# Layer-1 experts: the order of the layer-norm scales, who normalises the first tokens, and where the shared output is kept

## The chip, the cores and the metric

The kernel runs on one core of a Trainium2 chip. The metric is the time of one execution on the device in microseconds (us); three executions of the kernel before took 2908.03, 2914.95 and 2923.42 us, so its median is 2914.95 us. Engines are TensorE (PE; PEld is its weight load), VectorE (DVE), ScalarE (ACT), GpSimd (POOL) and SyncE (SP), whose queue issues most of the DMAs.

## The reference

Twelve sublayers work on `x`, 4096 tokens of 128 numbers in float32. The change touches the third kind, which is called twice, around the layer-1 attention:

```python
x = x + 0.5 * _L1_ffn_ref(_layernorm(x, axis=-1), ...)

logits = x @ router_w.T                        # 64 experts
probs = softmax(logits); topk_w, topk_ids = top_k(probs, 8); topk_w /= sum(topk_w)
pos = (how many earlier (token, choice) pairs went to the same expert)
valid = pos < 64                               # an expert takes its first 64 tokens
y = (silu(xb @ w_gate) * (xb @ w_up)) @ w_down # per expert, xb its 64 tokens
routed = segment_sum(y * topk_w)
shared = (silu(x @ ws_gate) * (x @ ws_up)) @ ws_down
return routed + shared
```

`_layernorm(x)` is `(x - mean) / sqrt(var + eps)` per token.

## The kernel before, in words

`l1_ffn` (L1057 to L1611) is one stage: each engine has its own program, ordered by hand, and engines wait for each other by semaphores. All of `x` stays in SBUF as `core.x`: 32 tiles of 128 tokens, in 8 chunks of 4 tiles. The stage runs in three parts.

**Choosing.** VectorE makes means and variances of all tokens (`ln_scales_dve`), GpSimd raises the variances to the power -0.5 chunk by chunk (`ln_scale_pool`, L162): chunks 0 and 1, then two iotas and twelve small memsets, chunks 2 and 3, two memsets (`table_rows`' pad and `zero`), chunks 4 to 7. For each chunk VectorE's `shift(c)` (L1287) makes the product -mean times scale; ScalarE's `normal(c)` (L1443) normalises four tiles with it; TensorE's `turn_x(c)` (L1520) transposes them; ScalarE's `keep_xnt(c)` (L1449) copies the result out; TensorE multiplies by the router (`logits`, L1532); VectorE's `choose(c)` (L1313 to L1322) finds the 8 largest of 64 logits per token, the shifted logits and a mask; ScalarE's `exp(c)` (L1454) takes the exponential of the chunk's shifted logits. The two loops, as written:

```python
for c in range(CHUNKS):            # VectorE
    if c + 2 < CHUNKS:
        shift(c + 2)
    choose(c)
for c in range(CHUNKS):            # ScalarE
    keep_xnt(c)
    if c + 2 < CHUNKS:
        normal(c + 2)
    if c:
        exp(c - 1)
```

**Listing and the shared expert.** VectorE finds each expert's first 64 tokens: eight rounds of `largest` over 512 keys, five elementwise steps (L1355 to L1364), eight rounds over 256 keys, and the row numbers, which end with `index_ready` (L1390). Beside it the other engines work the shared expert off, chunk by chunk: TensorE `shared_up_of`, ScalarE `up_kept_of`, GpSimd `gate_shared(c)` (L1242), TensorE `shared_down`, ScalarE `keep_shared(c)` (L1480) into `ysc`, and GpSimd `add_shared(c)` (L1247), which adds `ysc` to `core.x`.

**Pairs.** Routed rows are gathered by token (`gather`, L1261), multiplied by two experts' weights at a time, 32 pairs, and added by indirect DMAs (L1272) to four accumulators in DRAM, the regions of `acc_dram`. Before that SP fills regions 1 to 3 with zeros (L1199), stores the routing table (L1205) and, as the adds are done, stores `core.x` into region 0 in four pieces (L1209). GpSimd's first gather waits for `index_ready`, the table and all those stores. At the end the four regions are loaded and summed into `core.x`.

Of the kernel before, what the change touches and what calls it, by code (L numbers as in the profile page):

```python
# [12 lines left out]
P = 128  # L13
# [4 lines left out]
CT = 4  # L18
# [1038 lines left out]
def l1_ffn(core):  # L1057
# [3 lines left out]
    PAIRS = EXPERTS // 2  # L1061
    TOP = 8
    RING = 4
    HALF = TILES // 2
    ROUNDS = CAP // TOP
    GROUP = 4
# [5 lines left out]
    with stage(nc) as s:  # L1072
# [27 lines left out]
        sg = s.sb("sg", [F, 2, CW])  # L1100
        su = s.sb("su", [F, 2, CW])
        hsh = s.sb("hsh", [F, 2, CW])
        ysc = s.sb("ysc", [P, 2, CW])
        key = s.sb("key", [P, GROUPS_OF])
        key2 = s.sb("key2", [P, CAP, GROUP])
        found = s.sb("found", [P, CAP])
# [52 lines left out]
        shared_h = s.sig("shared_h")  # L1159
        shared_y = s.sig("shared_y")  # L1160
        shared_kept = s.sig("shared_kept")
        shared_added = s.sig("shared_added")
        rows_stored = s.sig("rows_stored")
        ring_loaded = [s.sig(f"ring_loaded{q}") for q in range(RING)]
        added, xg_loaded = s.pool_dmas(core)[0:2], s.pool_dmas(core)[2:2 + RING]
# [19 lines left out]
        @block.sync  # L1185
        def _(sp):
            for t, m in ((wr_raw, "router_w"), (wsgu, "ws_gate_up"), (wsd, "ws_down")):
                sp.dma_start(t[:, :], w[f"L1_ffn_{m}"]).then_inc(w_loaded.sem, 16)

            def load(n, q):  # L1190
                for t, m in ((wg, "w_gate"), (wu, "w_up"), (wd, "w_down")):
                    sp.dma_start(t[:, q, :, :], w[f"L1_ffn_{m}"].rearrange("(b n) i o -> n i b o", b=2)[bass.ds(n, 1)].rearrange("n i b o -> i (n b) o")).then_inc(ring_loaded[q].sem, 16)

            for q in range(RING):
                load(q, q)
            sp.wait_ge(zero_filled.sem, 2)
            for b in range(1, 4):
                for n in range(TILES // 8):
                    sp.dma_start(region_rows(b)[:, n * 8:(n + 1) * 8, :], zero[:, :, :]).then_inc(zeroed.sem, 16)  # L1199
            for b in range(4):  # L1200
                sp.dma_start(sums[b * ROWS + TOKENS:(b + 1) * ROWS, :], zero[0:CAP, 0, :]).then_inc(zeroed.sem, 16)
            sp.dma_start(table[TOKENS:ROWS, :], zero[0:CAP, 0:2, :].rearrange("p a d -> p (a d)")[:, 0:TW]).then_inc(zeroed.sem, 16)
            sp.wait_ge(exp_done.sem, exp_done.past(CHUNKS - 1))
            sp.wait_ge(sums_inverted.sem, 1)
            sp.dma_start(table[0:TOKENS, :].rearrange("(p t) d -> p t d", p=P), table_rows[:, :, :]).then_inc(rows_stored.sem, 16)  # L1205
            for q in range(4):
                tiles = slice(q * 8, (q + 1) * 8)
                sp.wait_ge(shared_added.sem, shared_added.past(2 * q + 1))
                sp.dma_start(region_rows(0)[:, tiles, :], core.x[:, tiles, :]).then_inc(zeroed.sem, 16)  # L1209

            with sp.Fori(0, PAIRS // RING - 1) as ring:
                for q in range(RING):
                    sp.wait_ge(y_done.sem, y_done.past(ring * RING + q))
                    load(ring * RING + q + RING, q)
            for u in range(2):
                sp.wait_ge(added[u].sem, 16 * PAIRS // 2)
            for q in range(4):
                tiles = slice(q * 8, (q + 1) * 8)
                for b in range(4):
                    sp.dma_start(acc[b][:, tiles, :], region_rows(b)[:, tiles, :]).then_inc(acc_loaded[q].sem, 16)  # L1220

        @block.gpsimd
        def _(pool):
# [3 lines left out]
            for j in range(GROUP):  # L1227
                pool.memset(bits[:, j:j + 1], 1 << (GROUP - 1 - j)).then_inc(counts_filled.sem, 1)
                pool.memset(bits_f[:, j:j + 1], float(1 << (GROUP - 1 - j))).then_inc(counts_filled.sem, 1)
                pool.memset(within[:, j:j + 1], float(GROUP - j)).then_inc(counts_filled.sem, 1)  # L1230
            ln_scales_pool(pool, core, s, range(2, 4))
            pool.memset(table_rows[:, :, D + EXPERTS + 1:TW], 0.0).then_inc(zero_filled.sem, 1)
            pool.memset(zero[:, :, :], 0.0).then_inc(zero_filled.sem, 1)
            ln_scales_pool(pool, core, s, range(4, CHUNKS))
            pool.memset(hp[:, :, :], 0.0).then_inc(hp_clear.sem, 1)

            def gate_shared(c):
# [3 lines left out]
                    pool.wait_ge(shared_y.sem, shared_y.past(c - 2))  # L1241
                pool.tensor_tensor(hsh[:, c % 2, :], sg[:, c % 2, :], su[:, c % 2, :], ALU.mult).then_inc(shared_h.sem, 1)  # L1242

            def add_shared(c):
                pool.wait_ge(shared_kept.sem, shared_kept.past(c))
                xc = rows(core.x, c * CT, CT)
                pool.tensor_tensor(xc, xc, ysc[:, c % 2, :].rearrange("p (a b) -> p a b", a=CT), ALU.add).then_inc(shared_added.sem, 1)  # L1247

            for c in range(CHUNKS):
                gate_shared(c)  # L1250
                if c:
                    add_shared(c - 1)
            add_shared(CHUNKS - 1)
            pool.wait_ge(index_ready.sem, 1)
            pool.wait_ge(rows_stored.sem, 16)
            pool.wait_ge(zeroed.sem, 16 * (3 * TILES // 8 + 5 + 4))

            def gather(n):
                if n >= RING:
# [21 lines left out]

        @block.vector
        def _(dve):
            def shift(c):
                tiles = slice(c * CT, (c + 1) * CT)
                dve.wait_ge(s.scale_ready.sem, s.scale_ready.past(c))
                dve.scalar_tensor_tensor(core.nmr[:, tiles], core.mean[:, tiles], -1.0, core.rstd[:, tiles],  # L1287
                                         ALU.mult, ALU.mult).then_inc(nmr_ready.sem, 1)
# [40 lines left out]
                    dve.drain()  # L1329

            ln_scales_dve(dve, core, s)
            shift(0)
            shift(1)
            constants()
            for c in range(CHUNKS):
                if c + 2 < CHUNKS:
                    shift(c + 2)
                choose(c)
            dve.tensor_tensor(top_exp[:, :, :], top[:, :, :], top[:, :, 0:1].to_broadcast([P, TILES, TOP]), ALU.subtract).then_inc(top_shifted.sem, 1)

            dve.wait_ge(grouped.sem, 1)
# [93 lines left out]
        def _(act):  # L1435
# [1 line left out]
            act.activation(wr[:, :], kt[:, 0, 0:EXPERTS], ACT.Copy).then_inc(wr_kept.sem, 1)  # L1437

            def normal(c):
                act.wait_ge(nmr_ready.sem, nmr_ready.past(c))  # L1440
                for j in range(CT):
                    t = c * CT + j
                    last = act.activation(table_rows[:, t, 0:D], core.x[:, t, :], ACT.Identity, bias=core.nmr[:, t:t + 1],  # L1443
                                          scale=core.rstd[:, t:t + 1])
                last.then_inc(xn_ready.sem, 1)
# [2 lines left out]
                act.wait_ge(tp_ready.sem, tp_ready.past(c))  # L1448
                act.activation(xnt[:, c, :], tp[:, c % 2, :], ACT.Copy).then_inc(xnt_ready.sem, 1)  # L1449

            def exp(c):
                act.wait_ge(shifted.sem, shifted.past(c))
                here = table_rows[:, c * CT:(c + 1) * CT, D:D + EXPERTS]
                act.activation(here, here, ACT.Exp).then_inc(exp_done.sem, 1)  # L1454

            normal(0)
            normal(1)
            for c in range(CHUNKS):
                keep_xnt(c)
                if c + 2 < CHUNKS:  # L1460
                    normal(c + 2)
                if c:
                    exp(c - 1)
            exp(CHUNKS - 1)
            act.wait_ge(top_shifted.sem, 1)
            act.activation(top_exp[:, :, :], top_exp[:, :, :], ACT.Exp).then_inc(top_exp_done.sem, 1)

# [7 lines left out]

            def keep_shared(c):
                act.wait_ge(shared_y.sem, shared_y.past(c))
                if c >= 2:
                    act.wait_ge(shared_added.sem, shared_added.past(c - 2))
                act.activation(ysc[:, c % 2, :], ly[:, c % 2, :], ACT.Copy, scale=0.5).then_inc(shared_kept.sem, 1)  # L1480

            for c in range(CHUNKS):
                up_kept_of(c)
# [2261 lines left out]
```

## Time and profile before

| what | value |
| --- | --- |
| median of three executions (lowest, highest) | 2914.95 us (2908.03, 2923.42) |
| span of the profiled execution, first to last instruction | 2904.8 us, 46677 instructions |
| own time of the profiled execution | not given apart from its span; the lowest run is 3.2 us above the span |
| busy in the span: PE, PEld, DVE, ACT, POOL | 77%, 59%, 60%, 38%, 29% |
| first call of the stage, choosing and listing | from 581 us to the first gather at 657.26 us |
| second call, the same parts | from 883 us to 956.67 us |
| mean granted TensorE clock | 0.854 of full speed |

Busy shares over the whole span say little about this stage, which is about a tenth of it up to the pairs. It is read from the timeline: an engine's rows in order of time, each with the idle time before it and what ended it.

### The profile page before, as it was taken

The page shows a single profiled execution, that of the slowest core. Times are in us where ns is not written, and L with a number is a line of the kernel's source. Part 1 is how long each engine was busy: PE and PEld are TensorE (multiplying, and loading weights), DVE is VectorE, ACT ScalarE, POOL GpSimd, SP SyncE. Part 2 cuts the span into 40 slices and gives each one's busy share as a digit, 9 for nine tenths or more (in the row PEclk, how much of TensorE's full clock was granted, in tenths as well). Part 3 has the DMA queues.
Part 4 walks back from the last instruction along what each step waited for, and adds up shares of the span by engine and source line. Part 5 has one row for each costly group of instructions (what it writes and reads, how often), then busy time and mean ns, then how long its engine had stood idle before and what let it go on. Part 6 is the DMA issues. An engine that isn't in the chain of part 4 may idle for free. (4 is left out here: it accounts for less than half of the span.)

```text
span 2904.8 us, 46677 instructions
## 1 busy us (share of the span) xinstructions
PE 2229.6 (77%) x13745; PEld 1703.0 (59%) x13746; DVE 1746.7 (60%) x4315; ACT 1105.2 (38%) x2728; POOL 852.2 (29%) x773
## 2 busy tenths in 40 slices
PE   4978959767477652377799972575999989989999
PEld 3865549746365540266466651464788745547887
DVE  5557965573477348860365568832566678855555
ACT  1753317541045101144444422353333356663332
POOL 2544525446413651276100010475000123201000
PEclk9998959965597556598899986797999989999999
DMA  4120001255604578165322237355000233310000
GB/s 154 40 62 2 1 35 41 62 182 122 181 5 175 112 182 163 35 124 119 92 60 57 47 94 139 73 121 119 1 0 0 63 72 93 91 40 5 7 7 12
DMA packets 282919, 217.01 MB, mean 75 GB/s; under 512 B 103107, under 2 KB 254448, under 8 KB 279696
## 3 DMA queue, kind: packets, MB, share of 16 engines
q1 hardware_dynamic: 248592, 181.06, 23.1%
q0 software_dynamic: 34176, 34.09, 7.2%
q8 instruction: 75, 1.23, 0.2%
q14 instruction: 76, 0.62, 0.1%
HBM read 148.95 MB, written 65.17 MB: 74 GB/s over the span
## 5 line engine op out<-in xcount | busy, mean ns | idle before, releaser
L162 POOL TENSOR_TENSOR fields<-ln_t,power 128x4 f32<-128x4 f32 x96 | 98.1, 1047 | 374.2 <-DVE ln_t L155 374.1
L3366 DVE TENSOR_REDUCE s_mx<-s_sa 128x2 f32<-128x512 f32 x256 | 165.3, 684 | 41.8 <-PE s_sa L3516 40.6
L3446 ACT ACTIVATE s_e<-s_sc 128x512 f32<-128x512 f32 x256 | 149.2, 600 | 85.8 <-PE s_sc L3535 83.0
L3112 PE MATMUL s_z<-s_t,s_mix_h 128*128 128x256 f32 x768 | 171.3, 379 | 0.0
L2017 POOL DMA_INDIRECT acc_dram<-s_yo,s_to_i x96 | 152.5, 1588 | 48.2 <-issue 26.7
L2005 POOL DMA_INDIRECT s_xg<-rows_dram,s_from_i x96 | 94.5, 985 | 223.7 <-DVE s_to_i L2138 195.6
L3112 PEld LDWEIGHTS s_z<-s_t,s_mix_h 128*128 128x128 f32 x768 | 146.0, 190 | 20.5 <-issue 1.0
L2322 PE MATMUL s_hu<-s_xgt,s_w 128*128 128x128 f32 x768 | 122.9, 308 | 8.9 <-issue 7.1
L191 PE MATMUL s_tp<-ident,xn 128*128 128x128 f32 x192 | 39.8, 345 | 109.2 <-DVE xn L181 107.3
L573 DVE SCALAR_TENSOR_TENSOR s_hs<-s_ha,s_b,s_sg 128x128 f32<-128x128 f32 x312 | 87.8, 344 | 50.4 <-issue 29.5
L3162 PE MATMUL s_z<-xnt,s_wt_w 128*128 128x512 f32 x256 | 116.6, 610 | 1.5 <-ACT xnt L197 1.5
L2322 PEld LDWEIGHTS s_hu<-s_xgt,s_w 128*128 128x128 f32 x768 | 103.7, 210 | 16.6 <-issue 10.4
L627 ACT ACTIVATE s_sg<-s_hg,s_b 128x128 f32<-128x128 f32 x312 | 88.9, 368 | 59.7 <-PE s_hg L719 59.1
L2332 PE MATMUL s_lp<-s_w,s_h 128*128 128x128 f32 x768 | 110.3, 290 | 0.9 <-ACT s_h L2227 0.4
L1272 POOL DMA_INDIRECT acc_dram<-s_yo,s_to_i x64 | 101.7, 1588 | 30.8 <-issue 17.5
L2227 ACT ACTIVATE s_h<-s_hu,s_b 128x128 f32<-128x128 f32 x384 | 109.1, 374 | 1.2 <-PE s_hu L2322 1.1
L197 ACT ACTIVATE xnt<-s_tp 128x512 f32<-128x512 f32 x56 | 33.5, 598 | 198.0 <-PE s_tp L191 160.8
L425 POOL DMA_INDIRECT y_dram<-s_xg,s_to_ids x78 | 76.8, 984 | 107.6 <-DVE s_xg L584 107.6
L415 POOL DMA_INDIRECT s_xg<-x_dram,s_ids x78 | 75.7, 971 | 99.1 <-DVE s_ids L546 72.5
L2443 POOL TENSOR_TENSOR s_rd<-s_rv,s_power 128x2 f32<-128x2 f32 x16 | 11.1, 696 | 314.5 <-DVE s_rv L2488 314.5
L2332 PEld LDWEIGHTS s_lp<-s_w,s_h 128*128 128x128 f32 x768 | 100.7, 204 | 2.7 <-ACT s_h L2227 2.7
L191 PEld LDWEIGHTS s_tp<-ident,xn 128*128 128x128 f32 x192 | 29.9, 186 | 121.1 <-DVE xn L181 108.3
(549 smaller groups left out, 6042.6 us busy)
## 6 DMA issues: line engine op xcount, KB each, us to landing
s_w<-in_L_ffn_W_dram SPq DMA_DIRECT2D x96, 256.0 KB, 3.0
acc_dram<-s_zero SPq DMA_DIRECT2D x32, 512.0 KB, 5.4
s_share<-share_dram SPq DMA_DIRECT2D x32, 512.0 KB, 6.0
fields<-acc_dram SPq DMA_DIRECT2D x16, 512.0 KB, 7.5
table_dram<-s_table_rows SPq DMA_DIRECT2D x2, 3136.0 KB, 10.5
s_wg<-in_L_ffn_w_gate_dram SPq DMA_DIRECT2D x64, 96.0 KB, 2.1
s_wu<-in_L_ffn_w_up_dram SPq DMA_DIRECT2D x64, 96.0 KB, 2.2
s_wd<-in_L_ffn_w_down_dram SPq DMA_DIRECT2D x64, 96.0 KB, 2.2
```

The costliest lines, as they stand in the source:

```text
L162: pool.tensor_tensor(core.rstd[:, tiles], core.ln_t[:, 2, tiles], core.power[:, 0:CT], ALU.pow).then_inc(s.scale_ready.sem, 1)
L627: last = act.activation(sg[:, u, cols], hg[:, u, cols], ACT.Sigmoid, bias=b1[:, bass.ds(e, 1), HB + f])
L1272: pool.indirect_dma_start(sums, bass.IndirectOffsetOnAxis(ap=to_i[:, n:n + 1], axis=0), yo[:, n % RING, :], None, compute_op=ALU.add).then ...
L2005: pool.indirect_dma_start(xg[:, n % RING, :], None, table, bass.IndirectOffsetOnAxis(ap=from_i[:, n:n + 1], axis=0)).then_inc(xg_loaded[n ...
L2017: pool.indirect_dma_start(sums, bass.IndirectOffsetOnAxis(ap=to_i[:, n:n + 1], axis=0), yo[:, n % RING, :], None, compute_op=ALU.add).then ...
L2227: last = act.activation(h[:, u, j, :], hu[:, u, j * P:(j + 1) * P], ACT.Gelu, bias=b1[:, j, n:n + 1])
L2322: last = pe.matmul(hu[:, u, j * P:(j + 1) * P], w1[:, n % RING, j, :], xgt[:, u, :], start=True, stop=True)
L2332: pe.matmul(lp[:, u, j * P:(j + 1) * P], h[:, u, j, :], w2_flat[:, first:first + P], start=j == 0, stop=False)
L3112: last = pe.matmul(bank(n)[:, o, :], weights[:, f, o * P:(o + 1) * P], src[:, f, :], start=f == 0, stop=f == HALF - 1)
L3162: pe.matmul(z[:, (2 * f + half) % 4, :], wt[m][:, 0, f * P:(f + 1) * P], core.xnt[:, u, :], start=True, stop=True).then_inc(up_done.sem, 1)
L3366: dve.tensor_reduce(mx[:, i, t, 2 * pairs:2 * pairs + 2], sa[:, n % 2, :, :], AX.X, ALU.max).then_inc(max_done.sem, 1)
L3446: act.activation(e[:, n % RING, :, :], sc[:, n % 2, :, :], ACT.Exp).then_inc(exp_done.sem, 1)
```

## The change

Five edits, all in `l1_ffn`; the line numbers of the changed kernel are 2 to 5 higher.

1. VectorE normalises chunks 0 and 1 itself (a `normal` on VectorE with `tensor_scalar`); ScalarE does chunks 2 to 7.
2. `shift(2)` and `shift(3)` stand before the first `choose`, `shift(4)` to `shift(7)` right behind the first two. GpSimd makes the scales of chunks 2 to 7 in one go, ahead of the two memsets.
3. ScalarE's exponentials are two instructions, for chunks 0 to 5 and 6 to 7, behind the loop.
4. `add_shared` is gone. `ysc` has four buffers instead of two, and SP stores each chunk of it into region 1 as that accumulator's first value; `keep_shared(c)` waits for the store of chunk c - 4.
5. `core.x` itself is stored into region 0 at the start, in one DMA behind the wait for the zeros; region 1 is no longer filled with zeros.

```diff
-            for b in range(1, 4):
+            sp.dma_start(region_rows(0), core.x[:, :, :]).then_inc(zeroed.sem, 16)
+            for b in range(2, 4):
...
-            sp.wait_ge(exp_done.sem, exp_done.past(CHUNKS - 1))
+            sp.wait_ge(exp_done.sem, exp_done.past(1))
...
-            for q in range(4):
-                tiles = slice(q * 8, (q + 1) * 8)
-                sp.wait_ge(shared_added.sem, shared_added.past(2 * q + 1))
-                sp.dma_start(region_rows(0)[:, tiles, :], core.x[:, tiles, :]).then_inc(zeroed.sem, 16)
+            for c in range(CHUNKS):
+                sp.wait_ge(shared_kept.sem, shared_kept.past(c))
+                sp.dma_start(region_rows(1)[:, c * CT:(c + 1) * CT, :],
+                             ysc[:, c % SHARED, :].rearrange("p (t d) -> p t d", d=D)).then_inc(shared_stored[c % SHARED].sem, 16)
...
-            ln_scales_pool(pool, core, s, range(2, 4))
+            ln_scales_pool(pool, core, s, range(2, CHUNKS))
...
-            ln_scales_pool(pool, core, s, range(4, CHUNKS))
...
                 gate_shared(c)
-                if c:
-                    add_shared(c - 1)
-            add_shared(CHUNKS - 1)
...
+            def normal(c):
+                dve.wait_ge(s.scale_ready.sem, s.scale_ready.past(c))
+                for t in range(c * CT, (c + 1) * CT):
+                    last = dve.tensor_scalar(table_rows[:, t, 0:D], core.x[:, t, :], core.mean[:, t:t + 1], core.rstd[:, t:t + 1],
+                                             ALU.subtract, ALU.mult)
+                last.then_inc(xn_ready.sem, 1)
...
-            shift(0)
-            shift(1)
+            normal(0)
+            normal(1)
             constants()
+            shift(2)
+            shift(3)
             for c in range(CHUNKS):
-                if c + 2 < CHUNKS:
-                    shift(c + 2)
                 choose(c)
+                if c < 2:
+                    shift(2 * c + 4)
+                    shift(2 * c + 5)
...
-            normal(0)
-            normal(1)
             for c in range(CHUNKS):
                 keep_xnt(c)
                 if c + 2 < CHUNKS:
                     normal(c + 2)
-                if c:
-                    exp(c - 1)
-            exp(CHUNKS - 1)
+            exp(0, CHUNKS - 3)
+            exp(CHUNKS - 2, CHUNKS - 1)
...
-                if c >= 2:
-                    act.wait_ge(shared_added.sem, shared_added.past(c - 2))
-                act.activation(ysc[:, c % 2, :], ly[:, c % 2, :], ACT.Copy, scale=0.5).then_inc(shared_kept.sem, 1)
+                if c >= SHARED:
+                    act.wait_ge(shared_stored[c % SHARED].sem, 16 * (c // SHARED))
+                act.activation(ysc[:, c % SHARED, :], ly[:, c % 2, :], ACT.Copy, scale=0.5).then_inc(shared_kept.sem, 1)
```

VectorE's order, from the last constant of the first call to its second choice, before (`fields<-mean,fields` is `shift`, the four rows from MAX on are one `choose`):

```order
L1307 TENSOR_SCALAR s_slot<-s_slot 128x1
L1287 SCALAR_TENSOR_TENSOR fields<-mean,fields 128x4
L1313 MAX s_top<-s_ly 128x8 x4
L1316 MATCH_REPLACE s_rest<-s_top,s_ly 128x64 x4
L1318 TENSOR_TENSOR s_table_rows<-s_ly,s_top 128x4x64
L1322 TENSOR_TENSOR s_mask<-s_rest,s_ly 128x4x64
L1287 SCALAR_TENSOR_TENSOR fields<-mean,fields 128x4
L1313 MAX s_top<-s_ly 128x8 x4
```

and in the change:

```order
L1309 TENSOR_SCALAR s_slot<-s_slot 128x1
L1289 SCALAR_TENSOR_TENSOR fields<-mean,fields 128x4 x2
L1315 MAX s_top<-s_ly 128x8 x4
L1318 MATCH_REPLACE s_rest<-s_top,s_ly 128x64 x4
L1320 TENSOR_TENSOR s_table_rows<-s_ly,s_top 128x4x64
L1324 TENSOR_TENSOR s_mask<-s_rest,s_ly 128x4x64
L1289 SCALAR_TENSOR_TENSOR fields<-mean,fields 128x4 x2
L1315 MAX s_top<-s_ly 128x8 x4
```

Two products now stand where one stood, so that `shift(3)` no longer waits behind `choose(0)`, nor `shift(5)` behind `choose(2)`.

GpSimd's order in the shared expert, before (`s_hsh` is the gate, `fields<-fields,s_ysc` the add):

```order
L1242 TENSOR_TENSOR s_hsh<-s_sg,s_su 96x512 x2
L1247 TENSOR_TENSOR fields<-fields,s_ysc 128x4x128
L1242 TENSOR_TENSOR s_hsh<-s_sg,s_su 96x512
L1247 TENSOR_TENSOR fields<-fields,s_ysc 128x4x128
L1242 TENSOR_TENSOR s_hsh<-s_sg,s_su 96x512
L1247 TENSOR_TENSOR fields<-fields,s_ysc 128x4x128
```

and in the change, from the head of the stage on:

```order
L162 TENSOR_TENSOR fields<-ln_t,power 128x4 x6
L1234 MEMSET s_table_rows 128x32x3
L1235 MEMSET s_zero 128x1024
L1236 MEMSET s_hp 96x512
L1243 TENSOR_TENSOR s_hsh<-s_sg,s_su 96x512 x8
L1256 DMA s_xg<-table_dram,s_from_i 128x196 x4
```

The eight adds are gone from between the gates; six scales stand ahead of the memsets instead of two.

## Rows read from the trace of the kernel before

**Rows 1.** The page's head: the profiled execution's span.

```profile
span 2904.8 us, 46677 instructions
```

**Rows 2.** Timeline, VectorE, choosing: start us, length us, instruction, [idle before it <- releaser].

```profile
591.61 0.62 DVE L1313 MAX8 s_top<-s_ly 128x8 f32<-128x64 f32 x4 [3.61 <-PE s_ly L1532]
...
594.03 0.62 DVE L1313 MAX8 s_top<-s_ly 128x8 f32<-128x64 f32 x4
...
600.07 0.63 DVE L1313 MAX8 s_top<-s_ly 128x8 f32<-128x64 f32 x4 [3.54 <-PE s_ly L1532]
...
618.55 0.42 DVE L1322 TENSOR_TENSOR s_mask<-s_rest,s_ly 128x256 bf16<-128x256 f32 x1
...
892.85 0.62 DVE L1313 MAX8 s_top<-s_ly 128x8 f32<-128x64 f32 x4 [3.63 <-PE s_ly L1532]
...
918.31 0.42 DVE L1322 TENSOR_TENSOR s_mask<-s_rest,s_ly 128x256 bf16<-128x256 f32 x1
```

**Rows 3.** Timeline, ScalarE, first call: normalising chunk 3.

```profile
594.15 1.65 ACT L1443 ACTIVATE s_table_rows<-fields 128x128 f32<-128x128 f32 x4 [2.91 <-DVE fields L1287]
```

**Rows 4.** Timeline, TensorE, second call: one chunk of choosing.

```profile
904.13 1.12 PE L1520 MATMUL s_tp<-ident,s_table_rows 128*128 128x128 f32 x4 [1.72 <-ACT s_table_rows L1443]
905.04 1.85 PE L1532 MATMUL s_ly<-s_wr,s_xnt_all 128*128 128x64 f32 x8
906.70 1.12 PE L1520 MATMUL s_tp<-ident,s_table_rows 128*128 128x128 f32 x4
```

**Rows 5.** Windows: stretch, its length, busy us (count) of PE, PEld, DVE, ACT, POOL, PEclk, DMA share, GB/s.

```profile
600.00:605.00 5.00, 3.17 (x16) 2.98 (x15) 4.60 (x30) 2.72 (x7) 0.00 (x0) 0.50 1.02 400
```

**Rows 6.** Timeline, head of the first call: first two scales, first eight normalisations.

```profile
583.13 2.05 POOL L162 TENSOR_TENSOR fields<-ln_t,power 128x4 f32<-128x4 f32 x2 [12.17 <-DVE ln_t L155]
...
585.56 3.17 ACT L1443 ACTIVATE s_table_rows<-fields 128x128 f32<-128x128 f32 x8
```

**Rows 7.** Timeline, first stage of the program: VectorE normalising beside GpSimd.

```profile
15.61 3.55 DVE L181 TENSOR_SCALAR xn<-fields,mean 128x128 f32<-128x128 f32 x8 [1.15 <-POOL fields L162]
...
17.08 0.94 POOL L400 MEMSET s_b<- 128x1024 bf16 x1
...
19.06 5.12 POOL L162 TENSOR_TENSOR fields<-ln_t,power 128x4 f32<-128x4 f32 x5
...
20.16 1.11 DVE L181 TENSOR_SCALAR xn<-fields,mean 128x128 f32<-128x128 f32 x4 [0.20 <-POOL fields L162]
```

**Rows 8.** Timeline, VectorE, first call: listing.

```profile
618.89 0.42 DVE L1339 TENSOR_TENSOR s_top_exp<-s_top 128x256 f32<-128x256 f32 x1
...
635.07 0.66 DVE L1355 CAST s_found_i<-s_found 128x64 int32<-128x64 f32 x1
635.80 2.76 DVE L1357 TENSOR_TENSOR s_bit_i<-s_found_i,s_bits 128x256 int32<-128x256 int32 x1
...
641.48 2.55 DVE L1364 SCALAR_TENSOR_TENSOR s_key<-s_bit_i,s_key 128x256 f32<-128x256 int32 x1
644.10 0.43 DVE L1325 MAX8 s_found<-s_key 128x8 f32<-128x256 f32 x1
```

**Rows 9.** Timeline, GpSimd, first call: gates, adds, first gather.

```profile
637.01 1.27 POOL L1247 TENSOR_TENSOR fields<-fields,s_ysc 128x512 f32<-128x512 f32 x1
638.62 1.26 POOL L1242 TENSOR_TENSOR s_hsh<-s_sg,s_su 96x512 f32<-96x512 f32 x1 [0.34 <-issue]
639.85 1.27 POOL L1247 TENSOR_TENSOR fields<-fields,s_ysc 128x512 f32<-128x512 f32 x1
...
657.26 1.06 POOL L1261 DMA_INDIRECT s_xg<-table_dram,s_from_i  x1 [11.51 <-DVE s_to_i L1390]
```

**Rows 10.** Timeline, ScalarE: the last shared output of the first call.

```profile
643.82 0.60 ACT L1480 ACTIVATE s_ysc<-s_ly 128x512 f32<-128x512 f32 x1 [2.09 <-PE s_ly L1547]
```

**Rows 11.** DMAs issued from 580 to 660 us: count, KB each, median us to landing.

```profile
table_dram<-s_table_rows SPq DMA_DIRECT2D x1, 3136.0 KB, 11.1
acc_dram<-fields SPq DMA_DIRECT2D x4, 512.0 KB, 3.1
```

More of the change, by code:

```diff
@@ L1063, in l1_ffn @@
     RING = 4
+    SHARED = 4
     HALF = TILES // 2
@@ L1102, in l1_ffn @@
         hsh = s.sb("hsh", [F, 2, CW])
-        ysc = s.sb("ysc", [P, 2, CW])
+        ysc = s.sb("ysc", [P, SHARED, CW])
         key = s.sb("key", [P, GROUPS_OF])
@@ L1161, in l1_ffn @@
         shared_kept = s.sig("shared_kept")
-        shared_added = s.sig("shared_added")
+        shared_stored = [s.sig(f"shared_stored{q}") for q in range(SHARED)]
         rows_stored = s.sig("rows_stored")
@@ L1242, in gate_shared @@
                 pool.tensor_tensor(hsh[:, c % 2, :], sg[:, c % 2, :], su[:, c % 2, :], ALU.mult).then_inc(shared_h.sem, 1)
[L1244 to L1247, printed above, removed]
             for c in range(CHUNKS):
                 gate_shared(c)
-                if c:
-                    add_shared(c - 1)
-            add_shared(CHUNKS - 1)
             pool.wait_ge(index_ready.sem, 1)
             pool.wait_ge(rows_stored.sem, 16)
-            pool.wait_ge(zeroed.sem, 16 * (3 * TILES // 8 + 5 + 4))
+            pool.wait_ge(zeroed.sem, 16 * (2 * TILES // 8 + 5 + 1))
+            for q in range(SHARED):
+                pool.wait_ge(shared_stored[q].sem, 16 * (CHUNKS // SHARED))
             def gather(n):
@@ L1439, in normal @@
             def normal(c):
-                act.wait_ge(nmr_ready.sem, nmr_ready.past(c))
+                act.wait_ge(nmr_ready.sem, nmr_ready.past(c - 2))
                 for j in range(CT):
@@ L1449, in keep_xnt, with exp @@
                 act.activation(xnt[:, c, :], tp[:, c % 2, :], ACT.Copy).then_inc(xnt_ready.sem, 1)
-            def exp(c):
-                act.wait_ge(shifted.sem, shifted.past(c))
-                here = table_rows[:, c * CT:(c + 1) * CT, D:D + EXPERTS]
+            def exp(first, last):
+                act.wait_ge(shifted.sem, shifted.past(last))
+                here = table_rows[:, first * CT:(last + 1) * CT, D:D + EXPERTS]
                 act.activation(here, here, ACT.Exp).then_inc(exp_done.sem, 1)
-            normal(0)
-            normal(1)
             for c in range(CHUNKS):
```

## The prediction

> **What bounds the kernel now.** I read the page's head for the span [rows 1], then the timeline of this stage engine by engine, since each call is a string of short dependent steps in which no engine's busy share tells anything. In the first part, choosing, VectorE is the last engine of each chunk, but it idles: two chunks are chosen back to back, 2.42 us apart (591.61 to 594.03), then it waits 3.5 us for TensorE's logits [rows 2]. From the first choice to the last mask the first call takes 591.61 to 618.97 = 27.4 us, the second 892.85 to 918.73 = 25.9 us [rows 2], 3.4 and 3.2 us a chunk. TensorE in turn waits for ScalarE's normalisation, and ScalarE sat idle 2.91 us for VectorE's product (L1287) [rows 3]. So it is a ring: the product of chunk 3 stands in VectorE's queue behind choice 0, which needs logits 0; the normalisation, the transposes and the logits of chunk 3 can't start before. It closes every two chunks.
>
> In the second part, listing, VectorE is the chain up to the first gather, which waits for its row numbers (11.51 us idle before it, ended by VectorE) [rows 9]. Here the view shows something else: a two-input step over 128x256 takes 0.42 us with GpSimd idle (L1339), but L1357 takes 2.76 and L1364 2.55 [rows 8]. L1357 starts at 635.80 and ends at 638.56; GpSimd's add ran from 637.01 to 638.28 and a gate stood right before it [rows 8, 9]. It ends 0.28 us behind the add, the length of its own work: it stood still while GpSimd had two instructions back to back and got in where GpSimd paused (0.34 us before 638.62) [rows 9]. The whole piece from L1355 to the next MAX8 takes 635.07 to 644.10 = 9.0 us [rows 8].
>
> **The change part by part.** *Head.* Before, ScalarE's first eight normalisations end at 588.73 [rows 6]. Now VectorE starts on the first four at 584.2, behind the first of two scales that take 2.05 from 583.13 [rows 6]. Four such instructions take 1.11 us [rows 7]. The second four may meet iotas and memsets: in the program's first stage eight took 3.55 instead of 2.2, held beside memsets [rows 7], so 1.3 us more at worst. They end between 586.4 and 587.8; I take the middle, 587.1, a gain of 1.6 us a call (0.9 to 2.3).
>
> *Order of the products.* The ring is cut: every product is done by the second choice. What paces a chunk then? VectorE's 2.42; TensorE's transposes and logits, 904.13 to 906.70 = 2.57 [rows 4], at half clock: 0.50 is granted, the 1.2 GHz level [rows 5]; ScalarE's 1.65 for four normalisations [rows 3] leaves 0.9 for copying out. I take TensorE's 2.57, since 0.50 is what this part shows; if TensorE, now busier, is granted more, VectorE's 2.42 rules. From the first choice to the second I estimate 3.8: ScalarE's copy of chunk 1 stands behind normalising chunk 2, which waits for a product behind the constants. So 3.8 + 6 x 2.57 + 2.42 = 21.6 us, instead of 27.4 and 25.9: gains of 5.8 and 4.3. With the head, 7.4 and 5.9, **13.3 us** for the two calls. With 2.42 it would be 15.1; with no change of pace 3.2.
>
> *Adds removed.* Sixteen GpSimd adds of 1.27 us [rows 9] go, each followed at once by a gate or the reverse. A gate needs ScalarE's copies of TensorE's products and no add, so the gates stay where they are, about 2.84 us apart (637.01 to 639.85 for an add and the next) [rows 9], with GpSimd idle more than half of that. L1355 to L1364 cost, uncovered, three times 0.42, two shorter steps and five gaps of 0.07 (644.03 to 644.10) [rows 8]: about 2.0 us. One gate (1.26) in the way makes it 3.3. Instead of 9.0 that is 5.8 us a call, **11.6 us** for two. Without any gate in the way it is 7.0 a call, with two 4.5; nothing, if the gates alone hold VectorE as long. A loss has no place here: work is only taken off GpSimd.
>
> *Moved at no cost, and their cover.* The zero buffer is made four scales (4 us by rows 6) later and the stores with it, one of `core.x` and eight zeros in SP's queue instead of twelve; only the first gather waits for them, 50 us later, and that is the cover; without it, 4 us. The exponentials run while the last two choices run on VectorE (4.8 us); twelve pieces of 128 at 0.41 [rows 3] are 4.9, so at most a tenth shows. The table's store is waited for by the first gather alone. Two waits are new. ScalarE's fifth copy waits for the first `ysc` store, which stands in SP's queue behind the table (11.1 us for 3136 KB [rows 11]); the fifth copy comes four chunks, 11.4 us, after the first, so it is late by under 1 us, and TensorE's shared products behind it are not on the chain. GpSimd's first gather waits for the last `ysc` store. The last copy ended at 644.42 [rows 10]; 7.4 earlier is 637.0. A store of 512 KB lands in 3.1 us [rows 11]; one of 256 KB is taken the same: 640.1. The row numbers are ready at 657.26 - 7.4 - 5.8 = 644.1. So 4 us of cover remain.
>
> **Sum.** 13.3 + 11.6 = 24.9 us off the span of 2904.8 [rows 1]: 2879.9. The page gives the profiled execution no time beyond its span; the median of the runs lies 10.2 above that, so I forecast 2914.95 - 24.9 = **2890 us**, 0.85% less.
>
> **The rivals.** *VectorE locked out at the head.* By this, each of the moved normalisations waits until GpSimd's list, eight scales of 1.0 us and the memsets, has no instruction left: 583.13 and 8.2 for the scales and, I estimate, some 2 for iotas and memsets, about 593.5. They end near 594.6 instead of 587.1: 7.5 us a call, which eats all of 13.3. Total 9.9, 2905 us. Against it: four normalisations took their 1.11 us in the middle of five scales in a row (20.16, inside 19.06 to 24.18) [rows 7]; for it, those held beside memsets [rows 7]. The Trainium skill's page "SBUF — State Buffer", section "Who interferes with whom", says that a VectorE instruction in a mode that uses both its ports, `tensor_scalar` among them, and any GpSimd instruction exclude each other for a whole instruction, whoever starts first; by that rule this rival is what happens. The trace agrees for adds, gates and memsets and disagrees for the scales, and the measurement decides: chance 0.06.
>
> *Gates hold VectorE as the pair did.* If L1357 to L1364 stand still as long behind the gates alone, nothing is gained there: 13.3 in all, 2901.7 us. For it: VectorE gets in only when GpSimd pauses; against it: pauses of 0.34 us were enough [rows 9], and now they exceed 1 us. Chance 0.09.
>
> *The change does not cut the ring.* If the pace is set by ScalarE's own order (copy, normalise, copy), a chunk still takes 3.3 us: 3.2 + 11.6 = 14.8, 2900 us. Against it: ScalarE's idle time was ended by the product, not by TensorE [rows 3]. Chance 0.06.
>
> *The last shared store ends the wait, and it is slower.* Past 644.1, each us by which that store lands later costs one us a call. Landing 11.1 us after issue, as the table does [rows 11], it is 648.1: 4 us a call, 2898 us in all. The kernel gets slower by over 0.5% only if the store takes 27 us: 637.0 + 27 is 19.9 past 644.1, twice 19.9 less 24.9 is +14.9, 2930 us. No store of this stage takes half of that. Chance 0.03.
>
> **How the numbers follow.** Half a per cent, 14.6 us, is about what a measurement of this kernel tells from no change. The forecast has 0.76; all of it is faster by more. The ring rival lies on the edge and is split. So faster 0.76 + 0.03 = 0.79, same 0.06 + 0.09 + 0.03 = 0.18, slower 0.03. The range: downwards 15.1 + 14.0 = 29.1 us of gain and the 7 us by which the lowest run lies under the median, 2879, rounded to 2877; upwards the gates' rival with its measurement, 2903. Outside lie the lock-out, the slower case and tails of the rest.
>
> **What would show it.** In the profile after: VectorE's eight normalisations end near 587 and the waits for logits from the second choice on shrink from 3.5 us to a few tenths, with choices 2.4 to 2.6 apart; the last mask ends near 611.5 and, in the second call, 912.8; L1357 and L1364 together take under 2 us instead of 5.3; the first gathers start near 644 and 945, released by VectorE's row numbers. Wrong would be: normalisations of over 1 us each beside the scales; ScalarE idle behind TensorE in the ring; one of the three steps still over 2 us; a first gather released by a DMA.

## The result, and the profile after

Four executions of the changed kernel have a median of 2883.15 us (2877.64 to 2888.25), four of the kernel before 2919.02 us. The ratio is 0.9892, with a 95% interval of 0.9871 to 0.9912: 1.1% faster, some 31 us (26 to 38); the two medians themselves stand 35.9 us apart. The forecast was 2890 us, 24.9 us less than the median then known.

The page's head of the changed kernel, which answers to [rows 1]:

```profile
span 2886.4 us, 46647 instructions
```

This span is only 18.4 us shorter, and that shortfall is not the change's doing. Outside the two calls nothing differs in the program, but one stage, `l3_attn`, takes 310.0 us here (2284.5 to 2594.5) and took 297.5 before (2315.8 to 2613.3). The views by windows of its last part, TensorE alone, show why (columns: stretch, length, busy us and count, granted clock, DMA share, GB/s). First the kernel before:

```profile
2500.00:2613.30 113.30, 101.43 (x984) 0.98 0.23 58
```

Then the changed kernel, with a narrow stretch inside:

```profile
2468.70:2594.50 125.80, 113.83 (x991) 0.88 0.22 52
...
2534.00:2540.00 6.00, 6.00 (x40) 0.50 0.10 19
```

The same products take 12.4 us more TensorE time because the granted clock lay at 0.50, the 1.2 GHz level, for a while. How long it does so differs between executions; over the 13 profiled executions of this study, what lies outside the two stretches named next varies from 2756 to 2771 us. I therefore measure each kernel from the first VectorE instruction of the stage (the first `ln_scales_dve` row) to the first gather: two stretches that hold the whole change and repeat within 0.8 us for the two kernels that were profiled twice. Before the change they are a twentieth of the span (not the tenth that the section on time before gives). They took 75.41 and 73.54 us before and take 59.71 and 59.04: 15.70 and 14.50, together **30.2 us** less, which fits the ratio.

VectorE's timeline after, choosing in the first call (answers to [rows 2, 6]):

```profile
586.02 2.25 DVE L1282 TENSOR_SCALAR s_table_rows<-fields,mean 128x128 f32<-128x128 f32 x8 [1.17 <-POOL fields L162]
...
591.15 0.63 DVE L1315 MAX8 s_top<-s_ly 128x8 f32<-128x64 f32 x4 [0.95 <-PE s_ly L1534]
...
594.51 0.62 DVE L1315 MAX8 s_top<-s_ly 128x8 f32<-128x64 f32 x4 [0.78 <-PE s_ly L1534]
...
597.01 0.61 DVE L1315 MAX8 s_top<-s_ly 128x8 f32<-128x64 f32 x4
...
599.41 0.63 DVE L1315 MAX8 s_top<-s_ly 128x8 f32<-128x64 f32 x4
...
611.13 0.42 DVE L1324 TENSOR_TENSOR s_mask<-s_rest,s_ly 128x256 bf16<-128x256 f32 x1
```

The waits of 3.5 us are gone; after the first, the choices stand 2.4 to 2.5 us apart. The same engine while listing (answers to [rows 8]), and GpSimd beside it [rows 9]:

```profile
627.64 0.19 DVE L1360 CAST s_found_i<-s_found 128x64 int32<-128x64 f32 x1
627.91 0.42 DVE L1362 TENSOR_TENSOR s_bit_i<-s_found_i,s_bits 128x256 int32<-128x256 int32 x1
628.25 0.19 DVE L1364 TENSOR_SCALAR s_group_i<-s_found_i 128x64 int32<-128x64 int32 x1
628.51 1.40 DVE L1366 TENSOR_TENSOR s_key<-s_group_i,s_within 128x256 f32<-128x256 int32 x1
629.99 0.42 DVE L1369 SCALAR_TENSOR_TENSOR s_key<-s_bit_i,s_key 128x256 f32<-128x256 int32 x1
630.49 0.43 DVE L1327 MAX8 s_found<-s_key 128x8 f32<-128x256 f32 x1
```

```profile
628.37 1.26 POOL L1243 TENSOR_TENSOR s_hsh<-s_sg,s_su 96x512 f32<-96x512 f32 x1 [1.36 <-ACT s_su L1476]
...
643.37 1.06 POOL L1256 DMA_INDIRECT s_xg<-table_dram,s_from_i  x1 [8.30 <-DVE s_to_i L1395]
```

One step of five is held, 1.40 instead of 0.42 us, by the gate of 628.37, which ends at 629.63: the step ends 0.28 us behind it. The first gather is still released by VectorE's row numbers.

### The profile page after: what moved, and what is told of

It is laid out like the page before. It is cut to its first block and busy times, and to the rows that moved or that the text cites. A ratio compares the mean times of both kernels' runs of the same rounds, so it can differ in the third digit from the quotient of the medians.

```text
span 2886.4 us, 46647 instructions
## 1 busy us (share of the span) xinstructions
PE 2232.8 (77%) x13745; PEld 1698.1 (59%) x13746; DVE 1739.1 (60%) x4327; ACT 1091.7 (38%) x2700; POOL 832.6 (29%) x757
## 6 DMA issues: line engine op xcount, KB each, us to landing
acc_dram<-fields SPq DMA_DIRECT2D x4, 2048.0 KB, 11.6
```

## The experiments

All kernels are read by the same five pieces, us in the first / second call: A from the stage's first VectorE row to the first choice, B on to the end of the last mask, C on to the CAST of the listing, D on to the next MAX8 (the piece with the five steps), E on to the first gather. (CAST converts a type; MAX8 finds the eight largest of a row.) The last column is the ratio to the kernel before, with its interval.

| kernel | A | B | C | D | E | sum | ratio |
| --- | --- | --- | --- | --- | --- | --- | --- |
| before | 9.76 / 9.72 | 27.36 / 25.88 | 16.10 / 16.10 | 9.03 / 9.04 | 13.16 / 12.80 | 75.41 / 73.54 | |
| the change | 7.49 / 7.45 | 20.40 / 20.05 | 16.09 / 16.10 | 2.85 / 2.63 | 12.88 / 12.81 | 59.71 / 59.04 | 0.9892 (0.9871 to 0.9912) |
| order_only | 7.49 / 7.45 | 20.05 / 20.06 | 16.11 / 16.45 | 8.35 / 8.67 | 12.88 / 12.82 | 64.88 / 65.45 | 0.9908 (0.9885 to 0.9931) |
| store_only | 9.66 / 9.62 | 27.37 / 25.88 | 16.10 / 16.09 | 2.85 / 2.85 | 13.18 / 12.82 | 69.16 / 67.26 | 0.9969 (0.9949 to 0.9990) |
| ring_back | 7.49 / 7.45 | 25.76 / 25.78 | 16.10 / 16.11 | 2.85 / 2.83 | 12.89 / 12.82 | 65.09 / 64.99 | 0.9902 (0.9874 to 0.9931) |
| act_first | 10.04 / 9.66 | 19.37 / 19.36 | 16.10 / 16.09 | 2.85 / 2.84 | 13.18 / 12.82 | 61.54 / 60.77 | 0.9910 (0.9880 to 0.9940) |
| exp_back | 7.48 / 7.45 | 21.55 / 20.55 | 16.10 / 16.23 | 2.56 / 2.98 | 12.88 / 12.82 | 60.57 / 60.03 | 0.9897 (0.9870 to 0.9925) |
| add_back | 7.49 / 7.44 | 20.39 / 20.40 | 16.10 / 16.24 | 8.37 / 8.90 | 12.88 / 12.82 | 65.23 / 65.80 | 0.9922 (0.9902 to 0.9942) |
| pow_back | 7.47 / 7.43 | 20.39 / 19.98 | 16.10 / 16.10 | 2.56 / 2.85 | 12.88 / 12.83 | 59.40 / 59.19 | 0.9885 (0.9864 to 0.9906) |
| group_first | 7.49 / 7.50 | 20.00 / 20.35 | 15.18 / 15.19 | 2.78 / 2.95 | 13.09 / 12.59 | 58.54 / 58.58 | 0.9870 (0.9852 to 0.9887) |
| change_again | 7.49 / 7.45 | 20.01 / 19.99 | 16.10 / 16.10 | 2.85 / 2.84 | 12.89 / 12.83 | 59.34 / 59.21 | 0.9875 (0.9857 to 0.9893) |
| early | 7.40 / 7.35 | 19.13 / 19.11 | 15.18 / 15.17 | 2.77 / 2.80 | 13.10 / 12.67 | 57.58 / 57.10 | 0.9866 (0.9844 to 0.9888) |
| early_again | 7.37 / 7.35 | 19.17 / 19.27 | 15.19 / 15.19 | 2.80 / 2.80 | 13.79 / 12.66 | 58.32 / 57.27 | 0.9875 (0.9855 to 0.9895) |

**order_only: edits 1 to 3 without 4 and 5.** Against the kernel before:

```diff
-            shift(0)
-            shift(1)
+            normal(0)
+            normal(1)
             constants()
+            shift(2)
+            shift(3)
...
-            exp(CHUNKS - 1)
+            exp(0, CHUNKS - 3)
+            exp(CHUNKS - 2, CHUNKS - 1)
```

> The kernel before with edits 1 to 3 alone (who normalises, the order of scales and products, the exponentials behind the loop); adds and stores as before. My theory: the two halves of the gain are separate, the ring of choosing and the hold of the listing. Then choosing goes as in the change (first choice 7.5 us after the stage's first VectorE instruction, last mask 20.4 us behind the first choice in the first call, 20.1 in the second) and the piece of listing from the CAST to the next MAX8 stays at 9.0 us. From the stage's first VectorE instruction to the first gather: 75.4 and 73.5 less 2.3 and less 7.0 and 5.8, so about 66.3 and 65.5; the kernel is about 17 us faster than before (0.6%). Rival: the faster choosing comes in part from the stores (12 zero stores are now 8, later adds gone); then the choices are more than 2.6 us apart and the gain is under 12 us.

The sums fall by 10.53 and 8.09, 18.6 us. Choosing (A, B) is that of the change, so it owes nothing to the stores; the listing (D) stays near 9. The theory holds for both halves; the rival falls.

**store_only: edits 4 and 5 without 1 to 3.** Against the kernel before:

```diff
-                if c:
-                    add_shared(c - 1)
-            add_shared(CHUNKS - 1)
...
-            for b in range(1, 4):
+            sp.dma_start(region_rows(0), core.x[:, :, :]).then_inc(zeroed.sem, 16)
+            for b in range(2, 4):
```

> The change without edits 1 to 3: choosing in the order of before, but no adds, four buffers for the shared output, stored as an accumulator's first value. My theory (VectorE's two-input steps are held while GpSimd has instructions back to back): choosing takes 27.4 and 25.9 us as before, the piece of listing 2.6 to 3.0 us instead of 9.0; from the stage's first VectorE instruction to the first gather 69.2 and 67.1 instead of 75.4 and 73.5; about 12.5 us faster (0.43%). Rival (the listing got shorter because it runs at another time against the gates, through edits 1 to 3): the piece stays over 5 us and the gain is under 8 us.

The sums fall by 6.25 and 6.28, 12.5 us, all but 0.2 of it in D; the theory holds. The two halves add up: 18.6 + 12.5 = 31.1 us, and together they gave 30.2.

**ring_back: the products back between the choices.** Against the change:

```diff
-            shift(2)
-            shift(3)
             for c in range(CHUNKS):
+                if c + 2 < CHUNKS:
+                    shift(c + 2)
                 choose(c)
-                if c < 2:
-                    shift(2 * c + 4)
-                    shift(2 * c + 5)
```

> The change with the products put back: the product of chunk c + 2 stands before choice c again. All else as in the change. My theory (the product that stands behind a choice closes the ring): choices come in pairs again, with waits of over 2 us for logits between pairs; first choice to last mask 26 to 27 us in the first call, 25 to 26 in the second, instead of 20.4 and 20.1; about 11 to 12 us slower than the change. Rival (ScalarE's exponentials within the loop set the pace, and they are gone): it stays under 22 us and the kernel is within 3 us of the change.

B grows by 5.4 and 5.7 us, 11.3 in the two sums: the size expected. The shape was not: no pairs with a long wait, but waits of 0.86 and 1.12 us in turn. VectorE's timeline of this kernel, and ScalarE's:

```profile
592.55 0.62 DVE L1315 MAX8 s_top<-s_ly 128x8 f32<-128x64 f32 x4 [1.13 <-PE s_ly L1531]
...
594.90 0.16 DVE L1289 SCALAR_TENSOR_TENSOR fields<-mean,fields 128x4 f32<-128x4 f32 x1
...
595.92 0.63 DVE L1315 MAX8 s_top<-s_ly 128x8 f32<-128x64 f32 x4 [0.86 <-PE s_ly L1531]
...
599.55 0.63 DVE L1315 MAX8 s_top<-s_ly 128x8 f32<-128x64 f32 x4 [1.12 <-PE s_ly L1531]
```

```profile
595.10 1.65 ACT L1445 ACTIVATE s_table_rows<-fields 128x128 f32<-128x128 f32 x4 [1.51 <-DVE fields L1289]
```

ScalarE waits for the product (594.90) that stood behind a choice, and two chunks take 7.0 us (592.55 to 599.55), as before the change (2.56 + 4.47 in the second call). The ring is what the new order of the products removed.

**act_first: the first two chunks normalised on ScalarE again.**

```diff
-            normal(0)
-            normal(1)
+            shift(0)
+            shift(1)
             constants()
...
+            normal(0)
+            normal(1)
             for c in range(CHUNKS):
                 keep_xnt(c)
```

The last lines are ScalarE's.

> The change with the first two chunks normalised on ScalarE again (products 0 and 1 before it). My theory: the first choice starts 9.8 us after the stage's first VectorE instruction instead of 7.5, and the rest is as in the change: 2.3 us a call, 4.6 us in all. Rival 1: the wait that follows the first choice in the change (3.4 us to the second, since ScalarE waits for the product of chunk 2 behind the constants) goes, so that part of it comes back and the cost is 1.4 us a call. Rival 2: VectorE gains nothing by normalising since it is held beside GpSimd's list: within 0.5 us a call of the change.

It costs 1.83 and 1.73 us a call: between the theory and rival 1. The first choice is 2.2 to 2.6 us later, but the second follows it by 2.50 us instead of 3.36, and B is 0.7 to 1.0 shorter. ScalarE normalises chunk 2 right behind its first copy there, while in the change it waits 1.11 us for VectorE's product, which stands behind the constants. Rival 2 falls.

**exp_back: the exponentials back in ScalarE's loop.**

```diff
+                if c:
+                    exp(c - 1)
-            exp(0, CHUNKS - 3)
-            exp(CHUNKS - 2, CHUNKS - 1)
+            exp(CHUNKS - 1)
```

> The change with ScalarE's exponentials back in the loop, one a chunk. My theory: ScalarE's turn for a chunk is copy and normalisation 2.02 us and exponential 0.35, 2.4 in all, just under TensorE's 2.45, so the pace stays; but in the first call the load of the exponential's table (1.28 us) stands in front of the copy of chunk 2 and delays TensorE's logits by 0.8 to 1.8 us, once. First choice to last mask 21.2 to 22.2 us in the first call instead of 20.4, 20.1 to 20.6 in the second. In all 1 to 2 us slower than the change. Rival (the exponentials set the pace): choices 2.8 us or more apart, 3 us a call.

B is 1.15 and 0.5 us longer, the sums 1.85 us in all, as the theory had it. In the first call one gap has 3.48 us instead of 2.5, and ScalarE's timeline shows what stands in it, ahead of the copy of chunk 2:

```profile
595.14 1.28 ACT L1459 ACT_TABLE_LOAD   x1
596.44 0.42 ACT L1459 ACTIVATE s_table_rows<-s_table_rows 128x256 f32<-128x256 f32 x1
596.76 0.58 ACT L1454 ACTIVATE s_xnt_all<-s_tp 128x512 f32<-128x512 f32 x1
```

The same load stood in the old loop, in the first call alone, and the first call's choosing (B) took 1.5 us more than the second's. ScalarE's timeline of the kernel before:

```profile
595.81 1.28 ACT L1454 ACT_TABLE_LOAD   x1
```

**add_back: adds on GpSimd again, for nobody.** They wait where the old ones did and write a spare tile. Against the change:

```diff
             for c in range(CHUNKS):
                 gate_shared(c)
+                if c:
+                    add_spare(c - 1)
+            add_spare(CHUNKS - 1)
...
+                pool.wait_ge(shared_kept.sem, shared_kept.past(c))
+                pool.tensor_tensor(spare[:, c % 2, :].rearrange("p (a b) -> p a b", a=CT), zero[:, 0:CT, :], zero[:, CT:2 * CT, :], ALU.add)
```

> The change with eight GpSimd adds of 128x512 put back behind the gates, into a spare tile that nobody reads; stores, buffers and choosing as in the change. My theory (GpSimd's adds and gates back to back hold VectorE's two-input steps): the piece of listing from the CAST to the next MAX8 takes 8 to 9.5 us again instead of 2.6 to 2.9; from the stage's first VectorE instruction to the first gather about 66 and 65 us instead of 59.7 and 59.0; 12 us slower than the change. Rival (the listing was held by the writes into x, its four stores or the ring of two buffers, not by GpSimd's engine): the piece stays under 4 us and the time is that of the change.

D is back at 8.37 and 8.90, the sums 12.3 us up. VectorE's timeline of the listing, then GpSimd's:

```profile
628.25 0.69 DVE L1335 MAX8 s_found<-s_key 128x8 f32<-128x512 f32 x1
...
633.14 2.48 DVE L1372 TENSOR_SCALAR s_group_i<-s_found_i 128x64 int32<-128x64 int32 x1
635.70 2.70 DVE L1374 TENSOR_TENSOR s_key<-s_group_i,s_within 128x256 f32<-128x256 int32 x1
638.48 0.42 DVE L1377 SCALAR_TENSOR_TENSOR s_key<-s_bit_i,s_key 128x256 f32<-128x256 int32 x1
```

```profile
627.57 1.27 POOL L1244 TENSOR_TENSOR s_hsh<-s_sg,s_su 96x512 f32<-96x512 f32 x1 [0.58 <-ACT s_sg L1483]
628.79 1.28 POOL L1248 TENSOR_TENSOR s_spare_add<-s_zero 128x512 f32<-128x512 f32 x1
...
633.01 1.33 POOL L1244 TENSOR_TENSOR s_hsh<-s_sg,s_su 96x512 f32<-96x512 f32 x1 [0.34 <-issue]
634.31 1.26 POOL L1248 TENSOR_TENSOR s_spare_add<-s_zero 128x512 f32<-128x512 f32 x1
635.63 1.26 POOL L1244 TENSOR_TENSOR s_hsh<-s_sg,s_su 96x512 f32<-96x512 f32 x1
```

A step of 0.19 us starts at 633.14 and ends at 635.62: it sat through a gate and an add and got in where the add ended (635.57). MAX8, with one input, takes its 0.69 us though all of it lies within a gate and the add behind it (627.57 to 630.07). So GpSimd's instructions themselves are enough to hold the listing; the writes into `x` and their stores, which this kernel lacks, are not needed for it.

**pow_back: a small power in the add's place.**

```diff
+                pool.wait_ge(shared_kept.sem, shared_kept.past(c))
+                pool.tensor_tensor(spare[:, c % 2, :], core.ln_t[:, 2, c * CT:(c + 1) * CT], core.power[:, 0:CT], ALU.pow)
```

> As the last one, with a power over 128x4 (some 1.05 us, almost no data) in place of each add of 128x512. My theory (it is GpSimd's traffic on the port that both engines share that holds VectorE, and the small power makes none for most of its time, as VectorE's normalisations beside the scales ran at full speed): the piece of listing stays at 2.6 to 3.6 us. Rival (any GpSimd instruction that runs shuts VectorE out for its whole length, as the Trainium skill's page SBUF — State Buffer has it in its section Who interferes with whom): 7 to 9 us, nearly as with the adds, since a power and a gate back to back leave VectorE as little room.

D is 2.56 and 2.85: what is held waits for a gate, as in the change, and nothing for a power. VectorE's timeline, then GpSimd's:

```profile
628.81 0.88 DVE L1368 CAST s_found_i<-s_found 128x64 int32<-128x64 f32 x1
629.76 0.42 DVE L1370 TENSOR_TENSOR s_bit_i<-s_found_i,s_bits 128x256 int32<-128x256 int32 x1
630.11 0.19 DVE L1372 TENSOR_SCALAR s_group_i<-s_found_i 128x64 int32<-128x64 int32 x1
630.37 0.42 DVE L1374 TENSOR_TENSOR s_key<-s_group_i,s_within 128x256 f32<-128x256 int32 x1
```

```profile
628.38 1.26 POOL L1244 TENSOR_TENSOR s_hsh<-s_sg,s_su 96x512 f32<-96x512 f32 x1 [0.38 <-issue]
629.60 1.00 POOL L1248 TENSOR_TENSOR s_spare_pow<-ln_t,power 128x4 f32<-128x4 f32 x1
```

The CAST waits for the gate's end (629.64); the next two run at full length inside the power (629.60 to 630.60), and the third starts inside it at full length. The Trainium skill's page "SBUF — State Buffer", section "Who interferes with whom", has the shared ports as a lock for a whole instruction, against VectorE instructions with two inputs in SBUF or in a two-port mode; that is narrower than the expectation has it, but TENSOR_TENSOR, with two inputs, falls under it. The traces agree for gates and adds, and for MAX8, which takes one input; they disagree for this power (TENSOR_TENSOR 0.42 us at 629.76). The power differs from the add in operation and in size, so which of the two frees VectorE stays open.

**early: two more moves on top of the change.**

```diff
-            ln_scales_pool(pool, core, s, range(2))
+            ln_scales_pool(pool, core, s, range(3))
...
+            shift(2)
             constants()
-            shift(2)
             shift(3)
...
-            shared_up_of(0)
             pe.wait_ge(chosen.sem, chosen.past(CHUNKS - 1))
...
             last.then_inc(grouped.sem, 1)
+            shared_up_of(0)
```

> The change with two more moves: GpSimd's scale of chunk 2 and VectorE's product of chunk 2 go ahead of the iotas and the constants, and TensorE's grouping products go ahead of the first shared products. My theory: ScalarE's third normalisation starts right behind its first copy (1.1 us sooner), TensorE no longer idles 0.65 us before the turn of chunk 2, and in the first call the keys start 0.45 us sooner after the last mask; 59.7 and 59.0 us to the first gather become about 58.6 and 58.4: some 1.7 us in all, 0.06%, seen in the trace and not in the times. Rival: the constants, now later, delay the first choice by up to 1 us and TensorE's logits of chunk 2 with it: no gain or a loss of under 1 us a call.

It gains 2.13 and 1.94 us, 4.1 in all, more than twice what was expected. B shrinks by 0.9 to 1.3 us, since ScalarE's third normalisation stands right behind its first copy now. And C, which is 16.1 in nearly every other kernel, is 15.2. The next run asks why.

**group_first: the grouping products moved alone** (the last part of the diff above).

> The change with one of the two moves alone: TensorE's grouping products go ahead of the first shared products. In five of the six profiles with the old place of the grouping the CAST of the listing starts 16.1 us behind the last mask in the first call, whether the keys start 0.7 or 1.3 us behind it. My theory: what sets it is not the keys but the first two gates, whose end the step on the sums (a TENSOR_SCALAR that makes the table's weights) waits for; with the shared products later these gates start behind that step, it takes 0.2 us instead of 0.5 to 1.2, and the CAST starts 15.2 us behind the last mask in both calls. The choices go as in the change (20.4 and 20.1 us). From the stage's first VectorE instruction to the first gather about 58.8 and 58.1. Rival (the 0.9 us came from the earlier scale and product, or from a higher clock): 16.1 as before.

C is 15.18 and 15.19 and the choosing is the change's own: the theory holds. (The keys are what VectorE makes first in the listing, from TensorE's grouping products.) The rows, first of the change (VectorE's step on the sums and GpSimd's first gates), then of this kernel:

```profile
616.78 0.63 DVE L1358 TENSOR_SCALAR s_table_rows<-s_wsum 128x32 f32<-128x32 f32 x1
...
614.87 2.49 POOL L1243 TENSOR_TENSOR s_hsh<-s_sg,s_su 96x512 f32<-96x512 f32 x2 [19.53 <-ACT s_su L1476]
```

```profile
617.44 0.20 DVE L1358 TENSOR_SCALAR s_table_rows<-s_wsum 128x32 f32<-128x32 f32 x1
...
617.86 1.26 POOL L1243 TENSOR_TENSOR s_hsh<-s_sg,s_su 96x512 f32<-96x512 f32 x1 [20.97 <-ACT s_su L1476]
```

In the change this step ends at 617.41, just behind the two gates (617.36), so keys that are ready sooner are lost in it. With the shared products later the step is done before the first gate. One more call bears it out: in the second call of order_only the gates end 6.16 us behind the last mask instead of 5.81, the step 6.22 instead of 5.86, and C is 16.45.

**change_again and early_again**, the two kernels beside each other.

> The change itself, on the same chip as the next one. Theory: 59.7 and 59.0 us to the first gather, and about 1% faster than before. What lies outside these two stretches varies by 15 us between profiled executions, so a repeated profile may have another span by as much.

> The change with both moves, again, beside the change on one chip: 57.6 and 57.1 us to the first gather, so 4.1 us less than the change in all, 0.14%: under what the runs can tell, and in the same direction if they tell anything. Rival: its lower median was the chip's other run-to-run differences, and it comes out within 2 us of the change or above.

The sums differ by 2.96 us (118.55 and 115.59), the ratios not at all: the extra moves are seen in the trace and can't be told in the times, and no claim is made for them beyond that. In its first call the version with both moves has 0.7 us more in E than in its earlier profile. In both, TensorE's product of the found rows stands directly behind the last shared products, and VectorE waits for it. The earlier profile has 1.16 and 0.45 us for them at a granted clock of 0.89 (637 to 640 us), the later one 1.60 and 0.69 at 0.61, and VectorE's wait is 1.68 us instead of 0.99.

## Why the prediction was right

**The mechanisms were those named.** The ring (ring_back), the late normalisation (act_first) and the hold by GpSimd's back-to-back instructions (add_back) each cost, put back alone, about what the prediction had given for its removal: 11.3 us in the two calls for the ring (10.1 forecast), 3.6 for the head (3.2), 12.3 for the adds (11.6). order_only and store_only show that choosing and listing are separate. One gain had no term of its own: the exponentials, which the prediction had as moved at no cost, gave 1.85 us (exp_back), and the forecast counted this with the ring, as it set the new pace against the whole old length of choosing. The four put back come to 29.0 of the 30.2 us. Nothing took their place: the fifth `ysc` copy of the first call waited 0.79 us for its store, "under 1 us" as said, and the first gather is released by row numbers. ScalarE's timeline after:

```profile
629.03 0.60 ACT L1482 ACTIVATE s_ysc<-s_ly 128x512 f32<-128x512 f32 x1 [0.79 <-DMA acc_dram<-s_ysc]
```

**The sum was 5.3 us too small, and every term erred the same way.** By calls, the pieces give 2.27 + 6.96 + 6.18 + 0.29 (C and E) = 15.70 us and 2.27 + 5.83 + 6.41 - 0.01 = 14.50. The 0.29 us of the first call were not forecast, and their cause stays open.

- *Head*: 1.6 us forecast, 2.27 measured. I took the middle between held and not held; the eight normalisations took 2.25 us, not held at all. The small memsets beside them lengthened instead: 0.11 to 0.24 us each, where they had taken 0.09. So the hold that I read from [rows 7] did not carry over to these.
- *Pace*: 21.6 us forecast for B, 20.40 and 20.05 measured. The first gap was 3.36, not 3.8. The 2.57 us came from [rows 4], a chunk whose transposes began after a wait; back to back it is 2.45 to 2.46, as TensorE's timeline of the first call shows:

```profile
594.26 1.06 PE L1522 MATMUL s_tp<-ident,s_table_rows 128*128 128x128 f32 x4
595.12 1.81 PE L1534 MATMUL s_ly<-s_wr,s_xnt_all 128*128 128x64 f32 x8
596.72 1.06 PE L1522 MATMUL s_tp<-ident,s_table_rows 128*128 128x128 f32 x4
```

  And TensorE was the pace only at the half clock. The windows of both calls, TensorE alone (columns: stretch, length, busy us and count, granted clock, DMA share, GB/s):

```profile
600.00:605.00 5.00, 5.00 (x27) 0.50 1.05 339
886.00:891.00 5.00, 3.40 (x28) 1.00 1.05 357
```

  In the second of them the clock is 1.00, TensorE idles, and the choices follow each other without a wait at VectorE's own 2.34 us, shorter than the 2.42 I read, which had a product in it (without one, the last two choices of the kernel before are 2.35 apart). VectorE's timeline of the second call:

```profile
887.12 0.62 DVE L1315 MAX8 s_top<-s_ly 128x8 f32<-128x64 f32 x4
...
889.46 0.61 DVE L1315 MAX8 s_top<-s_ly 128x8 f32<-128x64 f32 x4
```

- *Adds*: 5.8 us a call forecast, 6.18 and 6.41 measured. I charged a whole gate of 1.26; a step that meets a gate already running waits for its rest only (1.40 against 0.42).

**The times of the second call** were misstated: 912.8 for the last mask and 945 for the gather left out that this call starts earlier by what the first gains. With its gain of 13.2 they read 899.6 and 931.8; 896.55 and 928.09 were measured. That the marks of the first call fit (611.5 and 644 forecast, 611.55 and 643.37 measured) is in part luck: the stage began 1.81 us later in this execution (583.66, before 581.85), which hides most of what the sum was short of.

**The rivals.** VectorE was not locked out at the head; gates alone hold one step a call; the ring is cut; the store ends nothing. The remaining 1.6 us between the forecast and the median are not explained by the two stretches. The base does not explain them either: with its fourth execution the median of the kernel before rose by 4.1 us, to 2919.02. Executions of one kernel differ by more than that, 10.6 us after and 15.4 before.

## What to carry to other kernels

In a ring of engines, look for the small instruction that stands in a queue behind a large one which needs the ring's own result; here moving it ahead was worth 11.3 us in two calls. Steps like the TENSOR_TENSOR, SCALAR_TENSOR_TENSOR, TENSOR_SCALAR and CAST of this listing, where they are on the critical path, should not run while GpSimd has adds or products over 512 columns back to back: a step of 0.2 us took 2.5. Where other stages make the span vary by more than the change, compare the stretch that holds the change, from one fixed row to another.

## What was not expected

- C stayed at 16.1 us whether the keys started 0.7 or 1.3 us behind the last mask: a 0.2 us step, held until two gates ended, set it. A hold absorbs what is gained ahead of it.
- A GpSimd power over 128x4 runs 1.00 us beside VectorE without holding it; an add of 1.27 us holds the steps of the listing until it ends, but not MAX8.
- The load of ScalarE's exponential table (1.28 us) stood inside the ring in the first call alone.
- Granted clocks differ between executions of one kernel at the same place: the first call's choosing went at 2.45 us a chunk in the change's first profile (clock 0.50 from 591 to 611 us) and at 2.34 in its second (0.67 from 591.9 to 611.9).
